# A fused attention and ternary feed-forward kernel: both stages' loops written out as straight code, and the weight rounding shared out anew

## The reference

```python
q, k, v = layernorm(x) @ Wq, ctx @ Wk, ctx @ Wv        # 16 heads
q, k = rmsnorm(q, gq), rmsnorm(k, gk)                  # per head
x = x + tanh(g_xattn) * (softmax(q k^T / sqrt(128)) v) @ Wo

def weight_quant(w):                                   # one scale for a whole matrix
    scale = clip(mean(abs(w)), EPS, None)
    return clip(round(w / scale), -1, 1) * scale
def act_quant(a):                                      # 8 bits, a scale for each row
    s = 127 / clip(max(abs(a), axis=-1), EPS, None)
    return clip(round(a * s), -128, 127) / s
bit = lambda a, w: act_quant(a) @ weight_quant(w).T
h = layernorm(x)
out = x + tanh(g_ffn) * bit(silu(bit(h, w_gate)) * bit(h, w_up), w_down)
```

## Time and profile before

| what | value |
|---|---|
| median of the runs | 2459.53 us |
| the profiled execution's own time | 2462.24 us |
| its span, first to last instruction | 2460.4 us |
| PE busy | 2247.8 us, 91% |
| DVE / ACT / POOL busy | 75% / 65% / 53% |
| mean granted TensorE clock | 0.962 |

### The profile page before, as it was taken

One profiled execution on the slowest core, in us unless ns is written; L12 is line 12 of the kernel. 1 busy time (PEld: TensorE's weight loads), 2 busy tenths in 40 slices (PEclk: granted clock), 3 DMA queues, 4 the chain that ended last, 5 costly groups with the idle time before them and its releaser, 6 DMA issues. The chain is left out here.

```text
span 2460.4 us, 52723 instructions
## 1 busy us (share of the span) xinstructions
PE 2247.8 (91%) x16336; PEld 1575.7 (64%) x16336; DVE 1851.5 (75%) x4149; ACT 1598.7 (65%) x3326; POOL 1303.7 (53%) x1679
## 2 busy tenths in 40 slices
PE   3599999999899989998999989998999999859999
PEld 1377776767676757775676667676677777634444
DVE  4577777787678767876777768776777777759997
ACT  3567667777577757775666656675666667636666
POOL 4365656565555545555767666765677655300000
PEclk8799999999999999998999989999999999979999
DMA  6455566777677677766676757776776756555555
GB/s 199 106 109 116 117 116 131 133 137 130 115 130 139 128 124 125 141 124 115 123 147 124 136 119 133 145 130 135 122 144 123 139 109 115 111 152 132 139 139 126
DMA packets 920385, 318.47 MB, mean 129 GB/s; under 512 B 865024, under 2 KB 883232, under 8 KB 919840
## 3 DMA queue, kind: packets, MB, share of 16 engines
q1 hardware_dynamic: 920096, 315.00, 65.3%
HBM read 82.48 MB, written 19.40 MB: 41 GB/s over the span
## 5 line engine op out<-in xcount | busy, mean ns | idle before, releaser
L858 DVE TENSOR_TENSOR khat<-keys_ps,krs 128x512 f32<-128x512 f32 (+1 forms) x384 | 263.7, 687 | 330.9 <-POOL krs L1128 330.9
L1134 POOL TENSOR_TENSOR ksplit<-khat,ksplit 128x512 bf16<-128x512 f32 (+1 forms) x384 | 443.9, 1158 | 60.2 <-ACT ksplit L643 58.7
L1125 POOL TENSOR_SCALAR kvar<-kss 128x4 f32<-128x4 f32 (+1 forms) x384 | 80.2, 209 | 616.7 <-DVE kss L848 614.7
L1128 POOL TENSOR_TENSOR krs<-kvar,minus_half 128x4 f32<-128x4 f32 (+1 forms) x384 | 387.3, 1009 | 32.0
L663 ACT ACTIVATE early<-score_ps,nbias,qrs 100x361 f32<-100x361 f32 x512 | 331.0, 652 | 89.2 <-DVE nbias L876 87.3
L672 ACT ACTIVATE psplit<-early,rden 100x361 bf16<-100x361 f32 x512 | 305.7, 597 | 100.7 <-DVE rden L882 99.3
L23 PE MATMUL keys_ps<-wk_split,ctxT 128*128 128x512 bf16 (+1 forms) x768 | 301.1, 392 | 68.6 <-DVE khat L858 51.4
L648 ACT ACTIVATE ksq<-keys_ps 128x512 f32<-128x512 f32 (+1 forms) x384 | 229.0, 597 | 194.8 <-PE keys_ps L25 194.2
L888 DVE SCALAR_TENSOR_TENSOR psplit<-early,rden,psplit 100x361 bf16<-100x361 f32 x512 | 337.2, 668 | 8.8 <-ACT psplit L672 3.7
L643 ACT ACTIVATE ksplit<-khat 128x512 bf16<-128x512 f32 (+1 forms) x384 | 241.1, 628 | 145.4 <-DVE khat L858 123.8
L866 DVE TENSOR_REDUCE nmax<-score_ps 100x1 f32<-100x361 f32 x512 | 269.3, 526 | 44.3 <-PE score_ps L25 44.1
(11 more groups left out here) (136 smaller groups left out, 5334.5 us busy)
## 6 DMA issues: line engine op xcount, KB each, us to landing
w_raw<-in_ffn SPq DMA_DIRECT2D x96, 256.0 KB, 3.0
ctx_raw<-in_ctx SPq DMA_DIRECT2D x31, 256.0 KB, 3.1
xin<-in_x SPq DMA_DIRECT2D x32, 200.0 KB
xres<-in_x SPq DMA_DIRECT2D x32, 200.0 KB
x_rows<-xres SPq DMA_DIRECT2D x32, 200.0 KB
xin<-x_rows SPq DMA_DIRECT2D x25, 256.0 KB, 2.7
xres<-x_rows SPq DMA_DIRECT2D x25, 256.0 KB, 2.8
out<-xres SPq DMA_DIRECT2D x25, 256.0 KB, 2.0
```

What stands on the lines that cost most here:

```text
L858: dve.tensor_tensor(khat[0:KV[t], k, :].rearrange("p (h d) -> p h d", h=G), keys_ps[k][0:KV[t], :].rearrange("p (h d) -> p h d", h=G), rs, ...
L1128: pool.tensor_tensor(krs[0:KV[t], k, :], kvar[0:KV[t], k, :], minus_half[0:KV[t], 0:G], ALU.pow).then_inc(krs_done, 1)
L1134: pool.tensor_tensor(ksplit[0:KV[t], t, 1, :], khat[0:KV[t], (u + t) % 2, :], ksplit[0:KV[t], t, 0, :], ALU.subtract).then_inc(k_lo_done, 1)
```

## The change

1. `for i in range(PAIRS)`: all 16 pairs are straight code on every engine and SP, without register waits, branches, or the `..._passed` marks that went with them. The feed-forward `steps` writes out all 25 tiles.
2. The sum job lies in pairs 1 to 6, its sums stay in SBUF (`w_abs`), and the total over the partitions is one PE matmul with a matrix of ones (`weight_totals`, pair 7). `w_sums` in DRAM, its stores and loads, the `parts` load and the second computation of the scales are gone; `w_scale` lives on into the feed-forward stage.
3. The tern job stays in pairs 8 to 13. Its first instruction goes from POOL to ACT (`weight_chunk`, same place as the sum chunk), two stay on POOL.
4. On POOL the chunk of the odd unit u moves from before `split_ctx`, `key_scale(v + 2, 0)` and `query_scale` to behind them, ahead of `key_scale(v + 2, 1)`. The chunk of the even unit v stays where it was.
5. One more memset (`w_ones`, 128 x 128) stands at the start of POOL.

```diff
-            for i in range(SUM_LOOPS[0] * BODY):
+            for i in range(PAIRS):
                 for u in range(1, UNITS, 2):
-                    two_turns(i, u, False, i % BODY)
-            for loops, job in ((SUM_LOOPS, "sum"), (TERN_LOOPS, "tern")):
-                with eng.Fori(*loops) as j:
-                    for r in range(BODY):
-                        for u in range(1, UNITS, 2):
-                            two_turns(j * BODY + r, u, False, r, j, job)
...
+                    two_turns(i, u)
...
+            def load_chunk(i, u):
+                n, m = sum_chunk_of(i, u), tern_chunk_of(i, u)
+                if n is not None and n > 0:
+                    sp.wait_ge(w_summed, n)
+                if m is not None:
+                    sp.wait_ge(w_summed, MATRICES * CHUNKS)
+                    if m > 0:
+                        sp.wait_ge(w_rounded, m)
...
+            def store_chunk(i, u):
+                m = tern_chunk_of(i, u)
+                if m is not None:
+                    rows, cols = chunk_at(m)
+                    sp.wait_ge(w_rounded, m + 1)
+                    sp.dma_start(w_tern[rows, cols], w_out[:, :]).then_inc(w_tern_out, 16)
...
+            def weight_totals(i):
+                eng.wait_ge(w_part_done, 1)
+                eng.wait_ge(y_added, i * 2 + 1)
+                pe.matmul(y_ps[0][:, 0:MATRICES], w_ones[:, :], w_part[:, :], start=True,
+                          stop=True).then_inc(w_total_done, 1)
...
+            def weight_chunk(i, u):
+                n, m = sum_chunk_of(i, u), tern_chunk_of(i, u)
+                if n is not None:
+                    eng.wait_ge(w_raw_in, (n + 1) * 16)
+                    act.activation(w_raw[:, :], w_raw[:, :], ACT.Abs,
+                                   accum_out=w_abs[:, n // CHUNKS, n % CHUNKS:n % CHUNKS + 1]).then_inc(w_summed, 1)
+                if m is not None:
+                    k = m // CHUNKS
+                    eng.wait_ge(w_raw_in, (MATRICES * CHUNKS + m + 1) * 16)
+                    eng.wait_ge(w_inv_done, 1)
+                    act.activation(w_raw[:, :], w_raw[:, :], ACT.Copy, bias=ROUND,
+                                   scale=w_inv[:, k:k + 1]).then_inc(w_scaled, 1)
...
-                pool.tensor_scalar(w_raw[:, :], w_raw[:, :], w_inv[:, 0:1], ROUND, ALU.mult, ALU.add).then_inc(w_scaled, 1)
-                eng.wait_ge(w_scaled, n + 1)
...
+            def round_chunk(i, u):
+                m = tern_chunk_of(i, u)
+                if m is not None:
+                    eng.wait_ge(w_scaled, m + 1)
+                    pool.tensor_scalar(w_raw[:, :], w_raw[:, :], ROUND + 1.0, ROUND - 1.0,
+                                       ALU.min, ALU.max).then_inc(w_clipped, 1)
+                    if m > 0:
+                        eng.wait_ge(w_tern_out, m * 16)
+                    eng.wait_ge(w_clipped, m + 1)
+                    pool.tensor_scalar(w_out[:, :], w_raw[:, :], -ROUND, 1.0, ALU.add, ALU.mult).then_inc(w_rounded, 1)
...
         def steps(eng, step):
-            with eng.Fori(0, TURNS) as j:
-                for s in range(2):
-                    step(j * 2 + s, s, 4)
-            for t in range(2 * TURNS, TILES):
+            for t in range(TILES):
                 step(t, t % 2, TILES - 1 - t)
...
-            sp.dma_start(parts[:, :, :], w_sums.rearrange("a p -> (a p)").partition_broadcast(P)
-                         .rearrange("q (a p) -> q a p", a=3)).then_inc(parts_in, 16)
```

More of the change, by code:

```diff
@@ L332, in _ @@
             turn_probs(-1, UNITS + 1, 0), turn_probs(-1, UNITS + 1, 1)
[L334 to L362, removed]
+            def chunk_at(n):
+                return slice(n // CHUNKS * P, (n // CHUNKS + 1) * P), slice(n % CHUNKS * CHUNK, (n % CHUNKS + 1) * CHUNK)
@@ new lines, in load_chunk @@
+            def load_chunk(i, u):
[6 more added lines that the diff above has]
+                        sp.wait_ge(w_rounded, m)
+                if n is not None or m is not None:
+                    rows, cols = chunk_at(n if m is None else m)
+                    sp.dma_start(w_raw[:, :], w_ffn[rows, cols]).then_inc(w_raw_in, 16)
@@ L410, in turn @@
                             load_x(i + 1, b, xres, xres_in)
-            sp.sem_inc(w_sums_out, 16)
-            sp.sem_inc(w_tern_out, 16)
-            for i in range(SUM_LOOPS[0] * BODY):
+            for i in range(PAIRS):
                 for u in range(1, UNITS + 1):
-                    turn(i, u, False, i % BODY)
-            with sp.Fori(*SUM_LOOPS) as j:
-                for r in range(BODY):
[L420 to L430, removed]
+                    turn(i, u)
             sp.wait_ge(w_tern_in, 10 * 16)
@@ L781, in two_turns @@
                     keys_hi(i, v + 2, 2)
-                if job == "sum":
-                    sum_chunk(j, i, v, par * UNITS + v - 1)
+                weight_chunk(i, v)
                 if sv:
@@ L996, in two_turns @@
                     queries_lo(i, u, 0)
-                if u == 1 and par == 0 and job == "tern":
-                    weight_scale(j)
+                if i == TERN_PAIR - 1 and u == 1:
+                    weight_sums()
                 if ku:
@@ L1102, in _ @@
             first_turn(-1, UNITS)
-            for i in range(SUM_LOOPS[0] * BODY):
+            for i in range(PAIRS):
                 for u in range(1, UNITS, 2):
-                    two_turns(i, u, False, i % BODY)
-            for loops, job in ((SUM_LOOPS, "sum"), (TERN_LOOPS, "tern")):
-                with eng.Fori(*loops) as j:
-                    for r in range(BODY):
-                        for u in range(1, UNITS, 2):
-                            two_turns(j * BODY + r, u, False, r, j, job)
-            for i in range(TERN_LOOPS[1] * BODY, PAIRS):
-                for u in range(1, UNITS, 2):
-                    two_turns(i, u, i == PAIRS - 1, i % BODY)
+                    two_turns(i, u)
         @block.gpsimd
@@ L1252, in _, with ffn_block @@
             first_turn(-1, UNITS)
-            for i in range(SUM_LOOPS[0] * BODY):
+            for i in range(PAIRS):
                 for u in range(1, UNITS, 2):
-                    two_turns(i, u, False, i % BODY)
-            for loops, job in ((SUM_LOOPS, "sum"), (TERN_LOOPS, "tern")):
-                with eng.Fori(*loops) as j:
-                    for r in range(BODY):
-                        for u in range(1, UNITS, 2):
-                            two_turns(j * BODY + r, u, False, r, j, job)
-            for i in range(TERN_LOOPS[1] * BODY, PAIRS):
-                for u in range(1, UNITS, 2):
-                    two_turns(i, u, i == PAIRS - 1, i % BODY)
-def ffn_block(nc, x1, g_ffn, wk_split, wq_split, w_sums, out):
+                    two_turns(i, u)
+def ffn_block(nc, x1, g_ffn, wk_split, wq_split, wscale, out):
     TOK, DM = x1.shape
```

165 lines of the change are left out of this document (57 added, 108 removed).

## The result

The changed kernel takes 2372.37 us (median of 4 runs, 2369.99 to 2376.88) against 2457.59 us for the kernel before, measured beside it: a ratio of 0.9649, with a 95% interval of 0.962 to 0.9678. The forecast was 2376 us. The profiled execution took 2376.88 us, its span is 2375.1.

What follows compares the result with a forecast made beforehand. PE's own work was the bound, 123.7 us a pair nearly a floor. 9 x 123.7 + 6 x 125.2 = 1864.5 against 1946.8 saves 82.3; with 1.1 - 0.2, 83.2 off 2462.2 gives 2379.0, less 2.7: 2376 us, range 2361 to 2402.

Steps and rivals of the forecast that it cites:

- The split of the excess: Attention pairs over 123.7 us each: 39.6 sum loop ends, 32.7 tern job, 19.4 tern loop ends; sum 91.7 us.
- both boundary mechanisms: Attention iteration ends: the branch and the 4-byte store ahead of the `xres` stores; all 59.0 us go.
- The sum job and pair 7: Sum job moved to pairs 1 to 6: nothing; pair 7's total: between 0 and 2 us, taken as 0.
- The tern job: Pairs 8 to 13: 125.2 us a pair, 1.5 over straight, bounds 123.7 to 129.15; the 2.20 us wait goes.
- a late third `krs`: Tern pairs, POOL's key scale for the third key tile: 0.2 to 1 us late, four times a pair.
- one of its own signs: Pair ends: no POOL wait over 3 us for the context if the prediction is right.
- POOL's place: Tern pairs: odd chunk behind `qrs` lets `krs` and `qrs` come as in a straight pair, removing PE's 2.20 us wait.
- the even chunk's load: SP in tern pairs: load goes at about 708.7 instead of 707.57; 0.9 us to spare, or ACT stalls 0.8.
- The lock between DVE and POOL: Tern pairs: if DVE with two SBUF inputs and POOL exclude each other, the chunk's place counts as much as its length.
- Feed-forward: Feed-forward loop written out: PE already busy 165.00 of 165.00 us, so 0 change, bounds 0 to 2 us lost.
- Rival 4: Whole program: some 170 newly straight packets make it slower than before; 2495 us at 0.7 us a packet; chance 0.02.
- The feed-forward stage's start: Start of feed-forward: DVE no longer waits 1.40 us for `parts`; 1.1 us saved.

Runs made afterwards that it cites:

- the last variant: Changed kernel with context loaded first, pairs' first unit without tern chunk, and the odd chunk early (POOL's two instructions in the old place): 2369.48 us, ratio 0.964.

## Why the prediction was right

*The split of the excess.* It held as a sum: 83.8 us for 15 pairs where 82.3 were forecast. Inside it the shares were less clean than I put them. The iteration ends gave all of their 59 us, but I called them "both boundary mechanisms" and priced the branch at 4.3 us on SP plus 2.56 on PE; without the sums' traffic the loop costs 3.7 to 6.9 us an end. At a sum end the tiny store is the larger part: 8.1 us each in straight code. An estimate from the kernel without the sums' traffic, 34 of 59: loops kept and sums kept in SBUF would have had over half of the gain of the ends; that kernel was not run.

*The sum job and pair 7.* Nothing, as forecast: pairs 2 to 7, five of them with the sum chunk and one with the total, are at 123.35 us.

*The tern job.* 125.6 us a pair where I took 125.2, inside the bounds of 123.7 and 129.15. The number came out better than its reasons. The 2.20 us wait in unit 3 went, as forecast. But the 1.5 us a pair that I left over were to come from a late third `krs`, and of that little shows: PE waits for `khat` 4.3 us in the six tern pairs and 3.4 us in the eight pairs 0 to 7, some 0.3 us a pair more. The largest wait left is the one for `qvar`, 7.1 us in six pairs against 2.9 in eight, 0.8 us a pair more. It comes from the context that lands late (with the context first it is gone), and the prediction did not have that; one of its own signs, no wait of POOL over 3 us for the context, failed with 3.50. That both came to about the same time was luck.

*What the move is worth.* The prediction put the gain down to POOL's place, and my expectation for the kernel with all three instructions in the new place called the move most of it. The move alone is worth nothing (769.0 against 767.3 us); it changes which key scale is late. Taking the third instruction off POOL is what makes the new place fit: 1.67 us of work into 2.4 us of slack, where 2.7 us don't fit. Over six pairs of 123.7 (742.2), the excess was 32.7 us before; straight code with the old tern job has 25.1 (767.3), all three instructions in the new place 26.8 (769.0), the changed kernel 11.2 (753.4). So the step from the loops to straight code gives 7.6 us here, and the shorter list together with its place gives 13.9. Of the 7.6, some is traffic of the sums again: pairs 12 and 13, from which I took 5.45 us a pair for the tern job alone, get 2.9 us shorter when the loads of `w_part` go. In the old place two instructions don't fit either: up to 1.5 us of waiting for `xT_lo` in each pair of the last variant.

*SP.* I feared that the even chunk's load would come late for ACT. ACT never waited for `w_raw` in a tern pair. What was late was the context load at pair ends, behind the load of the next pair's first chunk, which the prediction didn't name: 5.2 us in all.

*The lock between DVE and POOL.* The prediction said that no row it showed decided it. The rows of the variant with the context first show DVE held twice, to 0.01 us. For these pairs of instructions the rule of the Trainium skill ("SBUF — State Buffer", section "SBUF: two separate sides"), that a DVE instruction with two SBUF inputs and a POOL instruction exclude each other for a whole instruction, agrees with this trace. It does not hold here for every POOL instruction: in the trace of the kernel before, 124 short executions of `nbias` lie wholly inside POOL's `krs` (L1128, 1.01 us) and 24 inside its first rounding instruction (L1177, 0.99 us by its median), so the measurement narrows the rule (the profiler's spans on POOL are rough). All 147 executions over 0.3 us of that trace end with a `ksplit` or `nat` of POOL; the only short ones inside such an instruction are seven that began within 0.02 us of its start. So the lock was there before as after, in straight pairs too, and how much of the tern pairs' rest it makes up, no run shows apart.

*Feed-forward.* 0, shown from both sides. *Rival 4's premise* was wrong from the start: it counted some 170 packets as new in straight code, but the attention loops were fetched in each iteration already (last section).

*The feed-forward stage's start.* 1.1 us as forecast. From the end of `mv` to `xin`, DVE needs 1.12 us after, 2.19 before (2179.25 to 2181.44). The timelines, after and then before:

```profile
2094.26 0.18 DVE L1470 BATCH_NORM_AGGREGATE mv<-st 128x2 f32<-128x6 f32 x1
2095.56 0.55 DVE L1475 TENSOR_SCALAR xin<-xin,mv,rstd 128x512 f32<-128x512 f32 x1 [1.11 <-POOL rstd L1344]
```

```profile
2179.07 0.18 DVE L1547 BATCH_NORM_AGGREGATE mv<-st 128x2 f32<-128x6 f32 x1 [0.15 <-DVE st L1544]
2181.44 0.55 DVE L1552 TENSOR_SCALAR xin<-xin,mv,rstd 128x512 f32<-128x512 f32 x1
```

## What to carry to other kernels

Cut a periodic kernel into windows of equal work and read the excess of each over the best one. Averaged over six windows this gave a bound within 0.5 us a window before anything was tried, though single windows scattered by 3 us; and it shows whether a loop's ends or its body cost. A store of a few bytes a partition is dear not by its own time but for all that is behind it in the queue, and moving it mostly chooses another victim (9.8 us won, where taking the sums' traffic out won 22 in the same six pairs): keep such a reduction on chip. If work must be squeezed into an in-order engine's list, its length against the slack decides, and moving it without shortening it can simply pass the wait to the next user.

## What the runs showed of the hardware

- With a DMA of 128 times 4 bytes in front of them, two 200 KB stores land 10 to 11 us after their issue instead of 3.4, in looped and in straight code alike.
- Straight code fetched less in all: 129 + 95 packets of instructions (2.89 MB) in the changed kernel against 134 + 155 (3.47 MB) before. The attention loops had been fetched anew in each iteration (108 packets in pairs 2 to 7, against 76 in straight code); only the two-tile feed-forward body was not. That the register and branch instructions make the difference is likely, but no run shows it.
- ACT's copy with scale and bias on 128 x 512 f32 takes 0.71 us, its `abs` 0.62.
- A DVE instruction of one element a partition with two SBUF inputs, 0.16 us by its median, took 0.80 us beside a POOL instruction of 128 x 512. Beside POOL's 128 x 4 `krs` it kept its short time.
